# Two swaps at the end of an FFN tile: the low part of x ahead of a transpose on VectorE, the rounding of h6 ahead of that of x on ScalarE

## What is computed

```python
x = x + 0.5 * ffn(layernorm(x))
x = x + attn(layernorm(x))          # causal, rotary, one head of 128
x = x + 0.5 * ffn(layernorm(x))

def ffn(xt):                        # 16 experts of 64, top 4, and a shared expert
    scores = sigmoid(xt @ gate_w.T)
    _, idx = top_k(scores + gate_b, 4)
    w = take(scores, idx); w = w / sum(w) * 2.5      # comb: the 16 weights, 0 where not chosen
    for e in range(16):
        h = silu(xt @ w13[e, :64].T) * (xt @ w13[e, 64:].T)
        y = y + comb[:, e] * (h @ w2[e].T)
    return y + (silu(xt @ w13_s[:64].T) * (xt @ w13_s[64:].T)) @ w2_s.T
```

## Time and profile before

| | |
|---|---|
| median of 3 runs | 824.28 us (822.69 to 825.72) |
| profiled execution | 824.23 us, its span 822.4 us, TensorE's granted clock 0.994 |
| TensorE matmul / weight load busy | 801.5 us (97%) / 655.8 us (80%) |
| VectorE / ScalarE / GpSimd busy | 724.6 (88%) / 595.5 (72%) / 612.0 us (74%) |
| first FFN, attention, second FFN | to about 300 us, to about 520 us, to the end |
| one full FFN tile | 18.65 us |

### The profile page before, as it was taken

How to read it: one execution, slowest core, us unless ns; L and a number is a source line. 1 busy time by engine, 2 the same in 40 slices (tenths; PEclk the granted TensorE clock), 3 DMA queues, 4 the chain that set the end, 5 groups by cost and what they waited for, 6 DMA issues and landing times. The chain is left out here.

```text
span 822.4 us, 15760 instructions
## 1 busy us (share of the span) xinstructions
PE 801.5 (97%) x4022; PEld 655.8 (80%) x4022; DVE 724.6 (88%) x2027; ACT 595.5 (72%) x1495; POOL 612.0 (74%) x560
## 2 busy tenths in 40 slices
PE   8899999999999999999999999999999999999998
PEld 6677777777777777899999999777777777777777
DVE  6789999999999989788888887799999999999886
ACT  6677777777776667676676666777777777776664
POOL 6677777777677678889898884476777777777674
PEclk9899999999999999999999999999999999999999
DMA  6557788877777746542334550656677667665643
GB/s 228 135 150 212 205 237 239 253 227 232 215 199 206 213 129 164 170 122 78 106 97 129 142 151 18 156 149 190 188 201 194 186 185 202 180 173 171 179 142 95
DMA packets 93480, 140.83 MB, mean 171 GB/s; under 512 B 10352, under 2 KB 39648, under 8 KB 93408
## 3 DMA queue, kind: packets, MB, share of 16 engines
q1 hardware_dynamic: 93408, 140.03, 60.5%
HBM read 112.67 MB, written 18.93 MB: 160 GB/s over the span
## 5 line engine op out<-in xcount | busy, mean ns | idle before, releaser
L633 POOL TENSOR_TENSOR h_l<-probT,h_h 128x512 fp32r<-128x512 f32 x254 | 327.5, 1295 | 160.9 <-ACT h_h L857 157.8
L1796 PE MATMUL bank<-xh,w_h 128*128 128x512 f32 x545 | 216.6, 397 | 4.4 <-DVE prob L1314 3.8
L1796 PE MATMUL bank<-xh,w_l 128*128 128x512 f32 x545 | 215.2, 395 | 0.0
L1796 PE MATMUL bank<-xl,w_h 128*128 128x512 f32 x545 | 215.1, 395 | 0.0
L857 ACT ACTIVATE h_h<-probT 128x512 fp32r<-128x512 f32 (+1 forms) x285 | 179.0, 628 | 43.0 <-DVE probT L1327 18.7
L920 ACT ACTIVATE bank<-bank 128x512 f32<-128x512 f32 x252 | 146.3, 580 | 80.9 <-PE bank L1796 78.2
L1324 DVE TENSOR_TENSOR probT<-prob,bank 128x512 f32<-128x512 f32 x255 | 172.6, 677 | 14.3 <-POOL h_l L633 2.3
L1314 DVE TENSOR_TENSOR prob<-bank,qkT 128x512 f32<-128x512 f32 x252 | 171.3, 680 | 13.9 <-ACT bank L920 11.8
L1796 PEld LDWEIGHTS bank<-xh,w_h 128*128 128x128 f32 x545 | 103.2, 189 | 33.5 <-DVE prob L1314 6.9
L1796 PEld LDWEIGHTS bank<-xh,w_l 128*128 128x128 f32 x545 | 103.1, 189 | 23.5
L1796 PEld LDWEIGHTS bank<-xl,w_h 128*128 128x128 f32 x545 | 103.1, 189 | 22.6
(11 more groups left out here) (143 smaller groups left out, 1333.6 us busy)
## 6 DMA issues: line engine op xcount, KB each, us to landing
qkT<-comb_rows SPq DMA_DIRECT2D x190, 256.0 KB, 5.2
qkT<-comb_rows SPq DMA_DIRECT2D x124, 128.0 KB, 2.9
rows<-comb_rows SPq DMA_DIRECT2D x28, 512.0 KB, 7.2
stage<-stage SPq DMA_DIRECT2D x64, 128.0 KB, 2.5
X<-in_x SPq DMA_DIRECT2D x16, 256.0 KB, 3.1
stage<-in_x_t SPq DMA_DIRECT2D x16, 256.0 KB, 7.0
x_t<-stage SPq DMA_DIRECT2D x16, 256.0 KB, 4.4
X<-x_rows SPq DMA_DIRECT2D x64, 64.0 KB, 5.6
```

Source lines behind the costliest of these rows:

```text
L633: nc.gpsimd.tensor_tensor(lo, f, hi.bitcast(F32), ALU.subtract).then_inc(done, 1)
L1796: return nc.tensor.matmul(dst, lhsT, rhs, start=start, stop=stop)
```

## The change

On ScalarE, in all tiles but the opening one, the rounding of h of unit 6 now stands ahead of the rounding of the x of tile T + 2. On VectorE the turn moves from behind unit 7's product to behind xl. No instruction is added, removed or resized, and every wait stays with its instruction.

```diff
@@ ScalarE, ffn_tile @@
-                    if j == (PAIRS if start else PAIRS - 1) and ahead:
+                    if start and j == PAIRS:
                         ffn_xh(T + 2, q, base)
                     if j >= (2 if start else 1):
                         ffn_h_hi(T, q, j - 1)
                     elif not first:
                         ffn_h_hi(T - 1, 1 - q, UNITS - 1)
+                    if not start and j == PAIRS - 1 and ahead:
+                        ffn_xh(T + 2, q, base)
@@ VectorE, ffn_tile @@
                     ffn_h(T, q, j)
                     if j == NB + 2 and t + 2 < TILES:
                         ffn_scale(T + 2, base)
-                    elif j == PAIRS - 1 and base and t + TURN_AHEAD < TILES:
-                        turn_x2(t + TURN_AHEAD, turned[q])
-                    elif j == PAIRS - 1 and not base and not first:
-                        ffn_turn(T - 1, back)
...
                 if t + 2 < TILES:
                     ffn_xl(T + 2, q)
+                if base and t + TURN_AHEAD < TILES:
+                    turn_x2(t + TURN_AHEAD, turned[q])
+                elif not base and not first:
+                    ffn_turn(T - 1, back)
                 if first_batch == 0:
                     attn_item(("xnT", 0), 0, 0, True)
                 ffn_h(T, q, PAIRS)
```

## The result

The changed kernel takes 816.44 us (median of 4 runs, 815.68 to 818.59) against 824.10 for the kernel before: the ratio is 0.9916, with a 95% interval of 0.9890 to 0.9941. The interval lies clear of 1: faster, by 7 us, and inside the range given. A second set of runs, on the same chip as the last experiments, gave 0.9918 (0.9903 to 0.9933).

A forecast was written before the change was run, and what follows sets the result against it. TensorE, busy 97% of the span, was taken as the bound, losing time waiting on xl. Gains of 10.3 + 0.7 less 1.9 made 9.1 us, from 824.23 to 815.1 us; range 812.4 to 818.6.

The forecast's parts named there:

- Where the time goes: TensorE at a tile's end: the router matmul waits for VectorE's xl, 0.42 us a tile to be had.
- Part 1: VectorE, xl ahead of the turn: removes TensorE's wait on xl, 0.43 us in each of 24 tiles, 10.3 us.
- Part 2: ScalarE, r_6 ahead of xh: l_6 comes earlier, costs nothing, and gives 0.7 us in two tiles without a turn.
- h_8: VectorE's shared-expert product: 0.20 us late for the second gate's weight load, giving back 0.08 a tile, 1.9 us.
- VectorE keeps up: VectorE's round sums to about 17.9 us, under the new 18.3, as xs is held by GpSimd's l_5.
- Rival 2: VectorE becomes the bound, xs taking 1.26 us whatever runs: loop 18.42 us, gain 5.8, 818.4 us; chance 0.12.
- the 1.26 that was to show it: Sign that the forecast is right: VectorE's xs still takes near 1.26 us after the change.
- rival 4: GpSimd's centring waits for late x_t transfers, some 0.55 us a tile, 13 us, giving 837; slower cases together 0.07.

The follow-up runs named there:

- the two halves: Two kernels, each against the kernel before: VectorE's swap (xl ahead of the turn) alone, ratio 0.9975; ScalarE's swap (r_6 ahead of xh) alone, ratio 0.9977.
- The half alone: Only ScalarE's swap, h of unit 6 rounded ahead of the x of tile T + 2, against the kernel before: 822.38 us, ratio 0.9977.

## Why the prediction was right, point by point

- **Where the time goes.** Confirmed: the wait of TensorE on xl, 0.42 us a tile, was the loss; it is gone in 24 of 26 places. The full tile fell from 18.67 to 18.36, the forecast was 18.31.
- **Part 1.** xl starts where the turn did, 0.61 behind h_7, and ends at 186.31; the router's weights are loaded at 186.36, 0.05 behind it, and the matmul is on time.
- **Part 2.** Confirmed by the two halves: without it each tile gives 0.30 back on l_6. With it, l_6 is early. Its own 0.7 us, for the two tiles that load a further x but have no turn, came out: between the first traces of before and changed, the two windows that start with their down matmuls are 0.34 and 0.35 shorter. The half alone measured 2.0 with an interval of 0.9 to 2.9, so it gives something elsewhere too, in tile 14 for one.
- **h_8.** The mechanism is right, both the 0.03 behind the turn and the load 0.05 behind h_8. The size was 0.08 us a tile and is 0.11: the load came 0.23 late instead of 0.20, and 0.12 of it was absorbed, as the two rows of before said. Moving the turn takes these 0.11 away.
- **VectorE keeps up.** Right, and for the reason given: with xs behind w_7 it takes 0.69 each time. Rival 2 falls. After the change xs took 1.16 us at the median, a little less than the 1.26 that was to show it: it starts later against l_5.
- **Transfers.** This is the term that was missing from the sum. I had them as a rival that decides between faster and slower, in every tile or in none. In fact the landing time scatters, and after the change the late end of the scatter reaches over the slack: it adds 1.7 to 2.3 us over the 20 full tiles of the changed kernel's two traces, against 0.2 in both of before, and in the first trace another 1.4 in the tile without a turn at 738. The mechanism is rival 4's, at 2 to 3 us where 9.1 would have eaten the gain. Its slack was priced with the landing time of all transfers of that line, 7.0; in before's full tiles it was 6.4 at the median, and the slack 0.8 instead of 0.5.
- **Sum.** 10.3 + 0.7 - 1.9 was 9.1 us; the ratio gives 6.9, and the two profiled spans differ by 5.6. Tile by tile, these 5.6 are, rounded, 4.9 from the 20 full tiles (20 x 0.32 less 1.5 more of late transfers), 0.7 from the two tiles of part 2, 0.4 from tile 2, 0.5 from the opening, and 1.8 from tile 14 (19.17 to 18.37) and the first of the second FFN (18.12 to 17.16). Lost again are 1.5 in the tile at 738 and 1.1 in the second of the second FFN. The 1.8 is more than the 0.7 that 24 x (0.43 - 0.08) has for two tiles; it came again between the second traces, and no run shows why. So the forecast was right in its mechanism and within its range, but 24 equal tiles is not what happened: a loss that the sum did not have and a gain that it had too small stand against each other, and that part is luck.

## What to carry to other kernels

When one engine does work for two others in order, put ahead what the bound engine waits for, and then look at once for the next thing it waits for: here a swap on VectorE alone gave a quarter of a percent, since waiting for a low part on GpSimd cost 0.3 us two matmuls on, and only with a second swap on ScalarE did the gain come. Price a new wait by how far the load comes behind its due time, not by the idle time printed. Once tiles get shorter, transfers that had landed "in time" on average need their scatter looked at, not their median; moving them in one queue helps only if nothing in front of them waits for a landing.

## What the runs showed of the hardware

- A VectorE product of two SBUF operands took 0.69 us by itself and at the median 1.26 us (before) and 1.16 us (changed) where it came while GpSimd was in a subtraction on SBUF operands. Across the traces of before and changed it ended 0.56 us behind GpSimd at the median and never less than 0.55 (205.54 to 206.10 before, 183.78 to 184.34 after). The Trainium skill, SBUF — State Buffer, section SBUF: two separate sides, describes this exclusion, and the trace agrees. Moving it by one place took 0.5 us off its duration, and VectorE's busy time in a full tile fell from 17.3 to 17.0 us.
- A 128x128 weight load that came 0.15 to 0.23 us behind its due time (the start of the matmul before) cost TensorE 0.03 to 0.11 us; one that came 0.42 late cost 0.30. In all of them 0.12 was absorbed. The router's load, 128x32, absorbed more: in before it came 0.64 late 26 times and cost 0.44, so 0.20 was absorbed, and the 0.12 should not be carried to loads of another size.
- One queue leaves little room: the same transfers with two of them moved forward cost 2% (16 us), because the queue stood for a landing.
- Left open: why the landing times scatter by 2 us, and why four places in the program are prone to it. No run changed the transfers' number or size, so this wasn't tried.
